# Attention with one q/k projection and its bias added by GpSimd, scan with SiLUs and convolutions at other units

## The reference

```python
x = L0_attn_inp
x = _layernorm(x + _L0_attn_ref(x, ...), axis=-1)     # selective scan
x = _layernorm(x + _L0_ffn_ref(x, ...), axis=-1)
x = _layernorm(x + _L1_attn_ref(x, ...), axis=-1)     # attention
x = _layernorm(x + _L1_ffn_ref(x, ...), axis=-1)

# the scan, in _L0_attn_ref
def step(h, t):
    delta_t, B_t, C_t, u_t = t
    dA = jnp.exp(delta_t[:, :, None] * A[None, :, :])
    dBu = delta_t[:, :, None] * B_t[:, None, :] * u_t[:, :, None]
    h = dA * h + dBu
    y = jnp.einsum('bds,bs->bd', h, C_t)
    return (h, y)
...
y = _selective_scan(x, delta, Bm, Cm, A)
y = y + x * D[None, None, :]
y = y * _silu(z)
out = y @ W_out

# the attention, in _L1_attn_ref
xr = x.reshape(*x.shape[:-1], d // 2, 2)
x1, x2 = (xr[..., 0], xr[..., 1])
rot = jnp.stack([-x2, x1], axis=-1).reshape(x.shape)
return x * cos + rot * sin
...
q = (x @ Wq.T).reshape(b, s, 2 * H, D)
k = (x @ Wk.T).reshape(b, s, 2 * H, D)
v = (x @ Wv.T).reshape(b, s, H, 2, D)
q = rope_rotate(q).reshape(b, s, H, 2, D)
k = rope_rotate(k).reshape(b, s, H, 2, D)
...
o1 = sdpa(q1, k1, vfull)
o2 = sdpa(q2, k2, vfull)
o = o1 - lam * o2
ms = jnp.mean(jnp.square(o), axis=-1, keepdims=True)
o = o * jax.lax.rsqrt(ms + EPS) * ln_w + ln_b
o = o * (1.0 - LAMBDA_INIT)
return o.reshape(b, s, e) @ Wo.T
```

## Time and profile before

| | |
|---|---|
| runs | 1057.01, 1061.86, 1060.2 us |
| median | 1060.2 us |
| profiled execution: own time | 1057.07 us |
| its span | 1055.2 us |
| PE busy | 914.8 us (87%) |
| DVE busy | 883.0 us (84%) |
| POOL busy | 787.4 us (75%) |
| ACT busy | 728.2 us (69%) |

### The profile page before, as it was taken

How to read it: one execution, slowest core, us unless ns; L and a number is a source line. 1 busy time by engine, 2 the same in 40 slices (tenths; PEclk the granted TensorE clock), 3 DMA queues, 4 the chain that set the end, 5 groups by cost and what they waited for, 6 DMA issues and landing times. The chain is left out here.

```text
span 1055.2 us, 14663 instructions
## 1 busy us (share of the span) xinstructions
PE 914.8 (87%) x4482; PEld 482.1 (46%) x4482; DVE 883.0 (84%) x1337; ACT 728.2 (69%) x1600; POOL 787.4 (75%) x560
## 2 busy tenths in 40 slices
PE   7697979897989798687777779999999998799995
PEld 2233434342434343234555555566666553355544
DVE  4799999999999999998886477788887873489996
ACT  3776868686868777554565447788788778687871
POOL 2799998989898989885777753667667535677762
PEclk9899999899999999899998899999999999899997
DMA  4762424343343424101500323232332400000001
GB/s 150 321 236 85 202 119 202 120 199 123 139 184 121 176 112 195 40 1 48 100 1 16 104 68 108 80 114 81 104 104 81 118 6 2 0 2 21 10 21 30
DMA packets 35168, 104.03 MB, mean 99 GB/s; under 512 B 3659, under 2 KB 22475, under 8 KB 24395
## 3 DMA queue, kind: packets, MB, share of 16 engines
q1 hardware_dynamic: 35095, 103.16, 28.3%
HBM read 93.84 MB, written 8.91 MB: 97 GB/s over the span
## 5 line engine op out<-in xcount | busy, mean ns | idle before, releaser
L610 PE MATMUL bank<-m_hC,ident 128*128 128x512 f32 x512 | 257.8, 627 | 61.1 <-POOL m_hC L568 22.8
L558 POOL TENSOR_TENSOR m_dBu<-m_du,m_Bt 128x1024 f32<-128x1024 f32 x128 | 299.2, 2353 | 11.7 <-DMA m_Bt<-bcd 11.0
L333 DVE TENSOR_TENSOR_SCAN bank<-bank,m_dBu 128x512 f32<-128x512 f32 x184 | 222.3, 1219 | 16.1 <-ACT bank L461 16.1
L1411 DVE TENSOR_REDUCE a_nm<-bank 128x2 f32<-128x512 f32 x256 | 169.3, 686 | 58.8 <-PE bank L1643 58.4
L610 PEld LDWEIGHTS bank<-m_hC,ident 128*128 128x128 f32 x512 | 93.9, 196 | 203.5 <-issue 111.1
L1580 ACT ACTIVATE late<-bank 128x512 f32<-128x512 f32 x256 | 147.4, 599 | 54.3 <-PE bank L1643 53.5
L461 ACT ACTIVATE bank<-m_delta,early 128x510 f32<-128x510 f32 x256 | 170.0, 677 | 0.3
L342 DVE TENSOR_TENSOR m_hC<-bank,m_Ct 128x512 f32<-128x512 f32 x184 | 123.1, 669 | 0.0
L568 POOL TENSOR_TENSOR m_hC<-m_hS,m_Ct 128x512 f32<-128x512 f32 x72 | 94.4, 1312 | 26.6 <-DVE m_hS L333 26.6
L458 ACT ACTIVATE bank<-m_zero 128x2 f32<-128x2 f32 x181 | 31.2, 173 | 115.1 <-DVE m_hC L342 114.6
L1643 PE MATMUL bank<-qs,ks 99*128 99x256 bf16 x512 | 99.0, 275 | 7.1 <-ACT late L1580 5.8
(11 more groups left out here) (217 smaller groups left out, 1790.7 us busy)
## 6 DMA issues: line engine op xcount, KB each, us to landing
m_Bt<-bcd SPq DMA_DIRECT2D x32, 1024.0 KB, 5.5
m_Ct<-bcd SPq DMA_DIRECT2D x32, 1024.0 KB, 6.4
qs<-parts SPq DMA_DIRECT2D x16, 576.0 KB
ks<-parts SPq DMA_DIRECT2D x48, 192.0 KB
parts<-a_part SPq DMA_DIRECT2D x32, 192.0 KB, 2.3
out<-x_all SPq DMA_DIRECT2D x8, 256.0 KB, 2.3
vx<-in_vrow SPq DMA_DIRECT2D x4, 256.0 KB
qs<-in_fill SPq DMA_DIRECT2D x1, 768.0 KB
```

Of the source, the lines that this page charges most:

```text
L333: nc.vector.tensor_tensor_scan(out, decay, dBu[:, g % RD], 0.0, ALU.mult, ALU.add).then_inc(scan_ready, 1)
L558: nc.gpsimd.tensor_tensor(dBu[:, g % RD:g % RD + CH], du[:, n % 2], Bt[:, s].unsqueeze(1).broadcast_to([P, CH, GTOK]), ALU.mult).then_inc( ...
L610: return nc.tensor.matmul(out, lhsT, rhs, start=start, stop=stop)
L1411: nc.vector.tensor_reduce(nm[:, slot % 2, q, 2 * pair:2 * pair + 2], s1[i % 2][:], AX.X, ALU.max, negate=True).then_inc(max_ready, 1)
```

## The change

In the scan, `conv(m, 0)` moves from unit 0 to unit 31 of the group before (for the first group, ahead of the loop), and `conv(m, 1)` from unit 2 to unit 0; the wait for `z_took` is loosened for c = 0 by one. `silus(m)` moves from unit 10 to 9, `gates(n)` from unit 6 to 13. The copies and transposes of the FFN's weights beside the last group move to later units by 2.

In the attention, the columns of Wq and Wk are ordered so that one half of the 128 columns holds the even members of the rotary pairs (q and k), and the other half the odd ones: qk has shape [128, 2 halves, 256], and a member's partner is at the same place of the other half. One projection step of two matmuls gives all. rc and rs are both taken of the whole of qk, and rot has two operations of half the size, a subtraction for half 0 and an addition for half 1. TensorE transposes straight from `x_all`, and `copy_x` is gone. The bias ln_b times W_o is the same for every row of x: it is computed once, at n = -1 (TensorE u = 9, ScalarE u = 10), and GpSimd adds it to the batch's rows of `x_all` at u = 4 of body n (`add_bias`), after the batch has been transposed and before its residual is taken. The bias matmuls at u = 12 and 13 are gone.

```diff
@@ scan, ScalarE
-            if i == 10:
+            if i == 9:
                 silus(m)
...
-                if i == 6:
+                if i == 13:
                     gates(n)
@@ scan, TensorE
-            wait(pe, z_took, CH * m)
+            wait(pe, z_took, CH * (m - 1) + 1 if c == 0 else CH * m)
...
             if i == 0:
-                conv(m, 0)
-            if i == 2:
                 conv(m, 1)
...
+            if i == 31 and m + 1 < GROUPS:
+                conv(m + 1, 0)
...
+        conv(0, 0)
@@ beside the last group
-            if i in (8, 13):
-                n = (i - 8) // 5
+            if i in (8, 15):
+                n = (i - 8) // 7
...
-            if i == 18:
+            if i == 20:
...
-            if i in (1, 6):
-                n = (i - 1) // 5
+            if i in (1, 8):
+                n = (i - 1) // 7
...
-            if i == 11:
+            if i == 13:
@@ attention, SyncE
-                    sp.dma_start(k.parts[i].rearrange("a p t -> p a t"), part[:, :, i, :]).then_inc(parts_out, 16)
+                    sp.dma_start(k.parts[i].rearrange("a (h p) t -> p (a h) t", h=2),
+                                 part[P // 2 * i:P // 2 * (i + 1)].rearrange("p a h t -> p (a h) t")).then_inc(parts_out, 16)
@@ attention, VectorE
             dve.wait_ge(out_done, m + 1)
+            dve.wait_ge(x_biased, m + 1)
@@ attention, GpSimd
-        def copy_x(m):
-            pool.wait_ge(f.norm_chain, m // 2 + 1 if isinstance(m, int) else GROUPS)
-            nc.gpsimd.tensor_copy(xin[:], k.x_all[:, bass.ds(TS * m, TS), :]).then_inc(x_ready, 1)
+        def add_bias(m):
+
+            pool.wait_ge(x_turned, m + 1)
+            pool.wait_ge(bias_copied, 1)
+            x = k.x_all[:, TS * m:TS * m + TS, :]
+            nc.gpsimd.tensor_tensor(x, x, bias[:].unsqueeze(1).broadcast_to([P, TS, P]), ALU.add).then_inc(x_biased, 1)
...
-            for dst, src, table in ((rc, qk[:, 0], cos), (rs, qk[:, 1], sin)):
-                last = nc.gpsimd.tensor_tensor(dst[:], src, table.unsqueeze(1).broadcast_to([P, 2, SEQ]), ALU.mult)
+            for dst, table in ((rc, cos), (rs, sin)):
+                last = nc.gpsimd.tensor_tensor(dst[:], qk[:], table.unsqueeze(1).broadcast_to([P, 2, SEQ]), ALU.mult)
...
-            nc.gpsimd.tensor_tensor(rot[:], rc[:], rs[:], ALU.add).then_inc(rope, 1)
+            nc.gpsimd.tensor_tensor(rot[:, 0], rc[:, 0], rs[:, 1], ALU.subtract)
+            nc.gpsimd.tensor_tensor(rot[:, 1], rc[:, 1], rs[:, 0], ALU.add).then_inc(rope, 1)
...
-                if u == (6 if lone(n) else 10) and has(n, 5):
-                    wait(pool, x_turned, n + 5)
-                    copy_x(n + 5)
+                if u == 4 and has(n, 0):
+                    add_bias(n)
@@ attention, ScalarE
-                if u in ((7, 9) if lone(n) else (5, 7)) and has(n, 4):
+                if u == (7 if lone(n) else 5) and has(n, 4):
...
+                if u == 10 and isinstance(n, int) and n == -1:
+                    act.wait_ge(bias_done, 1)
+                    nc.scalar.activation(bias[:], ma[:, 0:P], ACT.Copy).then_inc(bias_copied, 1)
@@ attention, TensorE
-                    pe.wait_ge(x_ready, m + 1)
+                    pe.wait_ge(f.norm_chain, m // 2 + 1)
...
-                        last = nc.tensor.transpose((mb if lone(n) else ma)[:, P * t:P * t + P], xin[:, t], ident)
+                        last = nc.tensor.transpose((mb if lone(n) else ma)[:, P * t:P * t + P],
+                                                   k.x_all[:, TS * m + t, :], ident)
...
-                if u in ((6, 8) if lone(n) else (4, 6)) and has(n, 4):
+                if u == (6 if lone(n) else 4) and has(n, 4):
...
+                if u == 9 and isinstance(n, int) and n == -1:
+                    pe.wait_ge(nmT_ready, 1)
+                    mm(ma[:, 0:P], lnb[:], wo_c[:]).then_inc(bias_done, 1)
...
-                    mm(ma[:, P * t:P * t + P], lnb[:], wo_c[:], True, False)
-                    last = mm(ma[:, P * t:P * t + P], oT[:, P * t:P * t + P], wo_w[:], False, True)
+                    last = mm(ma[:, P * t:P * t + P], oT[:, P * t:P * t + P], wo_w[:])
```

More of the change, by code:

```diff
@@ L1258, in attention_phase @@
     lnb = sb("lnb", [P, P])
-    xin = sb("xin", [P, TS, P])
+    bias = sb("bias", [P, P])
     xT = sb("xT", [P, SEQ])
-    qk = sb("qk", [P, 2, 2, SEQ])
+    qk = sb("qk", [P, 2, SEQ])
     rc = sb("rc", [P, 2, SEQ])
@@ L1300, in attention_phase @@
     lam_chain = sem("lam_chain")
-    x_ready = sem("x_ready")
+    bias_done = sem("bias_done")
+    bias_copied = sem("bias_copied")
+    x_biased = sem("x_biased")
     x_turned = sem("x_turned")
@@ L1699, in body @@
                     m = n + 3
-                    wait(pe, qk_ready, 2 * m + 2)
+                    wait(pe, qk_ready, m + 1)
                     wait(pe, oT_ready, min_group(n - 2, BATCH))
                     for t in range(TS):
-                        last = mm(mb[:, P * t:P * t + P], xT[:, P * t:P * t + P], wqkv[:, 4 * P:5 * P])
+                        last = mm(mb[:, P * t:P * t + P], xT[:, P * t:P * t + P], wqkv[:, 2 * P:3 * P])
                     last.then_inc(v_done, 1)
@@ L1737, in body @@
                     pe.wait_ge(nm_chain, 5 * (n + 1) + 5)
-                    wait(pe, qk_ready, min_group(2 * (n + 4) + 1, 2 * BATCH))
+                    wait(pe, qk_ready, min_group(n + 5, BATCH))
                     wait(pe, r_ready, n - 2)
@@ L1744, in body @@
                     last.then_inc(nm_turned, 1)
+                if u == 9 and isinstance(n, int) and n == -1:
+                    pe.wait_ge(nmT_ready, 1)
+                    mm(ma[:, 0:P], lnb[:], wo_c[:]).then_inc(bias_done, 1)
                 if u == 9 and has(n, -2):
                     pe.wait_ge(on_ready, n - 1)
-                    wait(pe, qk_ready, min_group(2 * (n + 5), 2 * BATCH))
                     wait(pe, v_ready, min_group(n + 4, BATCH))
@@ L2243, in by_dim, with half @@
         return w.T.reshape(DM, 16, 8).transpose(0, 2, 1).reshape(DM, DM)
-    def exchanged(w):
-        return w.reshape(DM, 4, 2, 16)[:, :, ::-1].reshape(DM, DM)
+    def half(w, n):
+        return by_dim(w).reshape(DM, 4, 2, 16)[:, :, n].reshape(DM, DM // 2)
     inv_freq = (1.0 / np.float32(10000.0) ** (np.arange(0, 8, 2, dtype=np.float32) / np.float32(8))).astype(np.float32)
-    freqs = np.repeat(np.arange(SEQ, dtype=np.float32)[:, None] * inv_freq[None, :], 2, axis=1)
-    sign = np.where(np.arange(8) % 2 == 0, np.float32(-1), np.float32(1))
-    table = {n: np.repeat(f(freqs) * s, 16, axis=1) for n, f, s in (("cos", np.cos, 1), ("sin", np.sin, sign))}
+    freqs = np.arange(SEQ, dtype=np.float32)[:, None] * inv_freq[None, :]
+    table = {n: np.tile(np.repeat(f(freqs), 16, axis=1), 2) for n, f in (("cos", np.cos), ("sin", np.sin))}
     row = lambda v: np.tile(v.reshape(1, -1), (P, 1))
     ablocks = {
-        "wqkv": np.concatenate([by_dim(i[a + "Wq"]), by_dim(i[a + "Wk"]), exchanged(by_dim(i[a + "Wq"])),
-                                exchanged(by_dim(i[a + "Wk"])), i[a + "Wv"].T], axis=1),
+        "wqkv": np.concatenate([half(i[a + w], n) for n in range(2) for w in ("Wq", "Wk")] + [i[a + "Wv"].T], axis=1),
         "wo": i[a + "Wo"].T,
```

25 lines of the change are left out of this document (10 added, 15 removed).

## The result

| | before | changed |
|---|---|---|
| median of six runs | 1059.24 us | 1046.87 us |
| lowest and highest | 1056.49, 1061.86 | 1045.91, 1050.4 |
| profiled execution: own time, span | 1057.07, 1055.2 us | 1046.28, 1044.5 us |
| start of the last of the scans | 474.62 | 464.20 |
| that start to the split of batch 3's maxima | 195.36 us | 189.49 us |

The ratio is 0.9891, with a 95% interval of 0.9877 to 0.9906: 12.4 us faster by the medians, where the sum said 12.0. The lower half of the table cuts the span at two marks that both traces have; "split" is VectorE's cast of the row maxima (L1420 before, L1426 after). The four parts were forecast as -10.6, -4.5, +5.5 and -2.4; they came as -10.4, -5.9, +5.5 and +0.1.

What follows compares the result with a forecast made beforehand. VectorE was taken to bound the scan, VectorE and ScalarE the attention, not TensorE. Terms -10.6 - 4.5 + 5.5 - 2.4 = -12.0 on 1057.1 gave 1045, 1048 on the median's basis; stated 1047 us, range 1038 to 1055.

Steps and rivals of the forecast that it cites:

- Scan: Scan, seven groups: moving SiLUs to unit 9 and gates to unit 13 removes VectorE's waits for exponentials, -10.6 us.
- replay of one group: Scan group at 152.4 re-timed with the new places: some 1.55 of 1.63 us of waits go, scan 15 0.08 late.
- the SiLU part alone going is -6.4: Scan: bound if only the 0.92 us wait before the second late exponential goes, in seven groups.
- ScalarE behind: Rival, scan: two ScalarE blocks still four units apart, half the gain returns as waits at scans 14 and 15; 1052, chance 0.15.
- Convolutions: Scan: convolutions moved a unit sooner cost nothing, ending near 154.7 with 3.0 us of cover before the second SiLU.
- FFN and attention side by side: 557 to 642 us: one projection step and one copy fewer shorten GpSimd's rotation waits, -4.5 us (-2.5 to -5.5).
- Attention: Batches 1 to 12: removed matmuls worth nothing; GpSimd's addition stalls L1427 about 0.5 us in 11 batches, +5.5 us.
- The rival without a lock: Attention: the addition falls beside reductions reading PSUM and costs nothing; 1041 to 1042 us, chance 0.20.
- The rival in which TensorE is the bound: Attention: removed projection and bias matmuls save 1.3 us in each of 12 batches, no addition cost; 1026 us, chance 0.06.
- the pairs of distances of the earlier trace: Attention: TensorE distances with and without projections, 7.70 against 7.95 and 4.14 against 4.14, so removed matmuls are worth nothing.
- Tail: Batches 12 to 15: output projections on the last chain lose their bias matmuls, -2.4 us (-0.5 to -2.5).
- The 2 us added for the median: Whole kernel: sum of 1045 for the profiled execution raised to 1047, since the median of three runs was 3.1 higher.

## Why the prediction came out right, and where it did not

**Scan, right.** -10.6 forecast, -10.4 in the trace, -10.6 in the run with this part alone. The replay of one group from the durations of the earlier trace rows carried it: the remainder forecast, 0.08 us at one scan, came as none. (Seven times the 1.55 us of the replay are 10.9 and not 10.6, a slip of no weight.) Its reason for the second wait, that the lead can't be won back in four units behind the gates, was only half of it: with the gates gone the wait of 0.92 us stays. Its bound was wrong: "the SiLU part alone going is -6.4" took the two waits for separate; alone the SiLUs give 0.6 us by the medians. ScalarE behind, with chance 0.15, fell: of VectorE's waits for it in a group only the small third one is left.

**Convolutions, right.** ScalarE did not wait for them; the wait of 1.68 us in the earlier trace rows, which came once a group, is left only in the last group (1.55 us). Their cover was forecast as 3.0 us, and the run without the move shows that there was none before it.

**FFN and attention side by side, too small.** -4.5 (down to -5.5) forecast, -5.9 measured, and -5.95 with the attention's part alone. GpSimd's waits for the qk copies are 7.0 us in 2 after 19.1 in 4, where I said about 13. Before, four rotations waited 0.54, 2.92, 7.35 and 8.34 us; now the first two don't wait at all, and the others wait 3.13 and 3.89.

```profile
POOL a_rc L1513 <- ACT a_qk L1611: 7.0, 2, 3.9
...
ACT a_qk L1611 <- PE bank L1655: 6.9, 4, 3.0
```

Most of this gain hangs on TensorE's work, and not on the second copy or the copy of x: with the projection twice over, and both copies still gone, 4.1 of the 5.9 us are lost again (one doubled row, at 620.01, took 3.29 us).

**Attention, right in sum, half so in its terms.** The mechanism named, L1433 standing for the addition, is shown by its duration and by the run in which the addition starts behind it. It is the exclusive lock that the Trainium skill describes ("SBUF — State Buffer", Who interferes with whom): the operation that comes second stands for the other's whole remaining time, which the 0.66 us of L1433 against 0.19 agree with. But the term was 0.5 us a batch, and it is 0.36: I left out that the cast ahead would be quicker by 0.11. From batch to batch this makes 2.5 us in the seven periods between two jumps. The remaining 3.0 came from two things that I had not in the sum. In body 2 (what the expectations call batch 1) the period is 18.57, where it was 16.84. The addition meets the split's first half there. Before the change, and then after it:

```profile
669.85 0.62 POOL L1528 TENSOR_TENSOR late<-late,a_rms 128x256 f32<-128x256 f32 x1
669.98 0.53 DVE L1420 CAST a_nmp<-a_nm 128x32 bf16<-128x32 f32 x1
670.54 0.19 DVE L1422 TENSOR_TENSOR a_nmr<-a_nm,a_nmp 128x32 f32<-128x32 f32 x1
```

```profile
653.56 0.62 POOL L1539 TENSOR_TENSOR late<-late,a_rms 128x256 f32<-128x256 f32 x1
653.69 0.52 DVE L1426 CAST a_nmp<-a_nm 128x32 bf16<-128x32 f32 x1
654.14 0.73 POOL L1506 TENSOR_TENSOR x_all<-x_all,a_bias 128x256 f32<-128x256 f32 x1
654.25 0.67 DVE L1428 TENSOR_TENSOR a_nmr<-a_nm,a_nmp 128x32 f32<-128x32 f32 x1
```

The cast stands for the head norm's product in both. What is new is that the subtraction stands for the addition: VectorE loses 0.48 us. TensorE waits 0.51 and 0.61 us for it, where it waited 0.21 and 0.16, and then runs at half its clock for most of 3.8 us. That leaves 1.73 - 0.48 = 1.25 us for the clock and what else follows from the delay; how it divides is not shown. With the projection twice over the same cast and subtraction stand as long (0.53 and 0.66 us), the clock doesn't fall, and this period is no longer than the others (17.32). The windows of the changed kernel and, in the second fence, of the first run with the addition behind the split:

```profile
654.00:658.40 4.40, 3.27 (x26) 2.04 (x24) 4.26 (x12) 3.72 (x9) 0.87 (x2) 1.00 0.52 134
658.40:662.20 3.80, 3.69 (x17) 1.47 (x18) 2.33 (x5) 1.69 (x4) 3.13 (x3) 0.55 0.51 156
```

```profile
657.30:661.10 3.80, 3.64 (x30) 1.21 (x29) 2.80 (x5) 1.88 (x4) 3.60 (x4) 1.00 0.51 152
```

A granted clock of 0.50, which the trace shows from 659 to 661, is the lower of its two levels, 1.2 GHz in place of 2.4; over the whole window it comes to 0.55. This drop is in every trace in which the addition stands directly behind the head norm and TensorE has the lighter load (five), and in none where the addition is moved, dropped, or the projection done twice. In body 10 the period is 17.88, 1.28 more, with the wait of 0.83 us for the rows of maxima. This one belongs to this execution: in the second trace of the changed kernel and in that of the attention's part alone the period is 16.9, and the whole stretch from batch 3's split to batch 12's comes to 154.27 us, +4.6 and not +5.5. So that the size came out as forecast is luck: an addition overpriced by 0.14 us a batch, and two jumps that the sum did not have. The step that failed here is that the sum has no term for what a delay does to TensorE's clock, and none for the changed form of the two transfers, which the prediction doesn't mention.

The rival without a lock fell: its 1041 to 1042 came only where the addition was moved or dropped. The rival in which TensorE is the bound fell as well: with both of its parts removed the batches are longer. And the pairs of distances of the earlier trace rows were the right view. In the changed kernel the second stretch, with its two bias matmuls gone, still takes 734.64 - 730.49 = 4.15 us, what it took before, and the first, 728.95 - 720.90 = 8.05, is longer by the 0.35 of the split.

**Tail, wrong.** -2.4 forecast, +0.1 measured. The removed matmuls did give something: from batch 15's split to the normalization of batch 14, 39.8 us where it was 40.9. It is lost at both ends: ahead, where the wait of 1.17 us at 837.76 lies, and from the last projection on:

```profile
890.32 0.98 PE L1655 MATMUL bank<-a_wo_w,late 128*128 128x128 f32 x4 [3.74 <-ACT late L1624]
...
905.09 1.23 PE L1655 MATMUL bank<-a_wo_w,late 128*128 128x128 f32 x4 [3.95 <-ACT late L1624]
```

The step that failed reads the removed matmuls of batches 12 to 15 as time on the chain, each at its clock of before. The last projection, in one row, takes 1.23 us now, where the work of before, twice as much, took 1.16: half the work at the lower clock. In the second run of the changed kernel the same row took 0.71. So this term has no fixed size. That execution lost more all the same: from batch 12's split to the end it has 237.0 us, with 3.1 us gone to the lower clock between two splits. Over all fourteen traces this stretch takes between 231.2 and 238.0 us, and the shortest of them, with the projection twice over, has the changed transfers. A term of 2.4 us was finer than the stretch itself is steady, and what decides its length stays open.

**The median.** The sum stood at 1045.1 for the profiled execution, which took 1046.3: 1.2 us too low. The 2 us added for the median over it were 0.6: 1.4 too high. The two errors cancelled each other, and that the median came within 0.2 us of the 1047 is luck.

## What to carry to other kernels

Before work is moved to an idle GpSimd, look at what VectorE does in those very microseconds: an operation with two SBUF inputs stood here until GpSimd's had ended (0.66 us in place of 0.19). The cure may be a wait that starts GpSimd's a microsecond later, beside operations that read PSUM, or to leave the work where it was, if that engine does it in time that it has anyway. An engine at 98% busy need not be the bound: compare the same distance in a batch that lacks the work. And two blocks that stand in the way of a third engine need not be worth their waits one by one: replay the group with both moved before pricing either.

## What the runs showed of the hardware that I had not expected

- Two transfers of 64 partitions x 6 rows of 512 bytes took 1.31 us to issue on SyncE, and 3.63 us until the load behind them could be issued; as 128 partitions x 3 rows 0.90 and 2.75.
- TensorE's clock fell to its lower level behind a stretch in which it worked 3.27 of 4.40 us. With 3.36 of 4.30 us in the same place (the run with the addition behind the split) it did not.
- The same happens in bodies 12 and 13 in some executions and not in others, of one and the same program too. In the second trace of the changed kernel:

```profile
845.95 1.94 PE L1655 MATMUL bank<-late,vx 128*32 128x512 f32 x8
...
848.78 1.94 PE L1655 MATMUL bank<-late,vx 128*32 128x512 f32 x8
```

  These rows take 1.07 us at the full clock. Six of the fourteen profiled executions have such a row there and eight don't; with the addition behind the split it cost 2.9 us in one of two, and in the changed kernel 3.1 us in one of two. Part of the spread of the runs may be this; what decides it stays open.
